# A perceiver's next latents: reads of their PSUM banks moved within VectorE's step, two operations moved to GpSimd, and six banks for the context's products

## The chip, the cores and the metric

The kernel runs on one core of a Trainium2 chip. The metric is the device time of one execution in microseconds (us). Five engines take part, each with its own queue of instructions that it works off in order: TensorE (PE, products, with its weight loads PEld), VectorE (DVE), ScalarE (ACT), GpSimd (POOL) and SyncE (SP, which here only issues transfers). They meet at semaphores: an instruction that has to wait holds up everything behind it in its own queue.

## The reference

Two layers of cross attention and feed forward. The change lies in the second layer's attention, a perceiver: eight batches, 512 latents each (the rows of x after layer 0), 16 heads of 64, a context of 77 rows per batch.

```python
xn = layernorm(x, ln_x_g, ln_x_b)             # context, 8 x 77 rows
ln = layernorm(latents, ln_l_g, ln_l_b)       # 8 x 512 rows of 512
q = ln @ Wq
kv = concatenate((xn, ln), axis=1) @ Wkv      # k, v of context and latents
sim = einsum('bhid,bhjd->bhij', q * scale, k) # masked on the context
out = einsum('bhij,bhjd->bhid', softmax(sim), v)
```

The latents are x plus the output of the feed forward of layer 0, `x2 = x + alpha @ vo + bo`, normalised twice in one go (the layernorm before the attention and the attention's own).

## The kernel before

The kernel is a row of stages; a stage ends before the next begins. Two of them matter.

**The latents stage** (`build_latents`, tiles named `la_`) normalises and transposes the context, computes K and V of the context for all batches, and makes the latents of batch 0 alone (`FIRST = 1`). Every product is made of three passes (high x high, high x low, low x high; lines 119 to 121), since each operand is kept as a high part and a low part: ScalarE copies the result from its PSUM bank rounded ("hi"), and VectorE subtracts that from the bank ("lo"), after which the bank is free. The loop runs over eight pairs of heads: two K products (24 passes of 308 columns), one or two V halves (12 passes of 512 columns), and after the first pair the sixteen transposes of batch 0's latents. `place` (L1381) says which of eight banks a product takes; `claim` makes TensorE wait for the bank's last reader. `Vst` holds one block of V's rows until it has been stored.

**The perceiver stage** (`build_perceiver`, tiles `pa_`) runs 512 steps: 8 batches x 16 heads x 4 tiles of 128 latents; four steps are a head. A step's chain is: scores on TensorE (L1946, L1948, into one of two S buffers), their minimum on VectorE (`least`, L2218), the exponential on ScalarE (L2085), the reciprocal of the sum on VectorE (L2214), and the probabilities scaled on GpSimd (L1875). A head's probabilities are transposed in the next head's steps (T0 to T4, L1959), split into PTh (ScalarE) and PTl (VectorE, L2135), and weigh V (L1975, L1976). Every engine's list is written out step by step, and the order of the code within a step is the order on the engine. Q, K and V of later heads are computed between the steps. Three banks W serve Q, K, V and all transposes: `claim` (L1889 on) takes the bank that was released longest ago and waits for VectorE's mark "read" of its last user.

Beside that the latents of the next batch are made tile by tile, 28 tiles in all. A tile begins every 12 steps, so at an even head (steps 0 and 24 of a batch) or at an odd one (12 and 36). With n0 the step at which it begins: TensorE computes x2 at the end of step n0 (`residual`, L1984); VectorE adds it to x and measures at n0 + 1 (L2185, L2187, L2191); GpSimd makes the inverse root at n0 + 2 (L1881, L1883); VectorE normalises at n0 + 3 (L2196); TensorE transposes at the end of n0 + 4 (L1992); VectorE scales and shifts the result at n0 + 5 (L2202, four pieces); ScalarE rounds it at n0 + 6 (L2118); VectorE makes the low part at n0 + 7 (L2208); ScalarE's queue stores both. In VectorE's step this work stood last:

```python
for late, work in ((-1, ones), (1, add_and_measure), (3, normalised), (5, scaled), (7, latent_low)):
    if tile_at(n, late) is not None:
        work(tile_at(n, late))
```

Of the kernel before, what the change touches and what calls it, by code (L numbers as in the profile page):

```python
# [16 lines left out]
ALU = mybir.AluOpType  # L17
# [1310 lines left out]
def build_latents(nc, orders, a, x1_s, alphaT_s, vo_s, x2_s, z_s, Kc_s, Vc_s, Wkv, ahead):  # L1328
# [15 lines left out]
    with ExitStack() as ctx:  # L1344
# [12 lines left out]
        z_hi, z_lo = two("z_hi", [P, C, T], F32R), two("z_lo", [P, C, T], F32R)  # L1357
# [4 lines left out]
        Vst = sb("V", [P, PAIRS * 2, 2 * HD], F32R)  # L1362
# [7 lines left out]
        K_out, V_out = [sem(f"K_out{m}") for m in range(2)], sem("V_out")  # L1370
# [4 lines left out]
        for n in ("x", "l"):  # L1375
# [5 lines left out]
        place = {"x2": lambda b, t: t, "zT": lambda b, c: 3 + (b * C + c) % 3, "cT": lambda c: 3 + c % 3,  # L1381
                 "cT last": lambda: 4, "K": lambda q, h: 6 + h, "V": lambda k, h: 6 + h}
# [10 lines left out]
        def v_parts(k, h):  # L1393
            r = rows_of(k)
            src = bank_of["V", k, h][0:r, :].rearrange("p (h r d) -> p h r d", r=2, d=HD)
            to = Vst[0:r, h * VH:(h + 1) * VH, :].rearrange("p (h r) (x d) -> p h (r x) d", r=2, d=HD)
            return src, to[:, :, 0:4:3, :], to[:, :, 1:3, :]
# [3 lines left out]
        @block.sync  # L1401
        def _(sp):
            def load_small(b):
                m = b % 2
                sp.dma_start(aT[m][0:NS, :], alphaT_s[b]).then_inc(aT_in[m], 16)
                sp.dma_start(vo[m][0:NS, :], vo_s[b]).then_inc(vo_in[m], 16)

            def keys_out(q):
                for z in range(2):
                    sp.wait_ge(*(act_s, dve_s)[z].after(("hi", "free")[z], "K", q, 1))  # L1410
                    sp.dma_start(Kc_s[z][q], f32(Kst[z][q % 2][:, :])).then_inc(K_out[q % 2], 16)

            def values_out(k):
                sp.wait_ge(*dve_s.after("free", "V", k, 1))
                sp.dma_start(Vc_s[k * P:k * P + rows_of(k), :], f32(Vst[0:rows_of(k), :, :]).rearrange("p h d -> p (h d)"))\
                  .then_inc(V_out, 16)

            load_small(0)
            for dst, src in smalls:
                sp.dma_start(dst, src).then_inc(small, 16)  # L1420
            for b in range(FIRST):
                sp.wait_ge(*dve_s.after("free", "x2", b, NT - 1))
                sp.dma_start(x2_s[b:b + 1].rearrange("b (t p) d -> p (b t) d", p=P), X[b]).then_inc(x2_out[b], 16)
            for b in range(PAIRS):
                keys_out(b)
                for q, h in [i for i in v_of(b) if i[1]]:
                    values_out(q)
            for b in range(FIRST):
                sp.wait_ge(x2_out[b], 16)
            for m in range(2):  # L1430
                sp.wait_ge(K_out[m], 16 * PAIRS)
            sp.wait_ge(V_out, 16 * KT)
# [81 lines left out]
        def _(act):  # L1514
# [30 lines left out]
            for b in range(PAIRS):  # L1545
# [6 lines left out]
                for k, h in v_of(b):  # L1552
                    act.wait_ge(*pe_s.after("V", k, h))
                    if k:
                        act.wait_ge(V_out, 16 * k)
                    src, hi, _ = v_parts(k, h)
                    act.activation(hi, src, ACT.Copy).then_inc(*act_s.mark("hi", "V", k, h))
# [80 lines left out]
def build_perceiver(nc, orders, a, x1_s, alphaT_s, vo_s, x2_s, z_s, Kc_s, Vc_s, o_s, xs_s, mask_s, Wq, Wkv, Wout_s):  # L1638
# [26 lines left out]
    with ExitStack() as ctx:  # L1665
# [188 lines left out]
        def _(pool):  # L1854
# [16 lines left out]
            for n in range(STEPS):  # L1871
# [7 lines left out]
                if i is not None:  # L1879
# [3 lines left out]
                    pool.tensor_tensor(lrstd, lve, minus_half, ALU.pow).then_inc(*pool_s.mark("x2 rstd", i))  # L1883
            low_part(PAIRS - 1)

        @block.tensor
        def _(pe):
# [99 lines left out]
            def latent(i):  # L1987
                u = ("zT", i)
                claim(u)
                pe.wait_ge(*dve_s.after("xn", i))  # L1990
# [37 lines left out]
        def _(act):  # L2028
# [52 lines left out]
            for n in range(1 - LEAD, STEPS + 2 * NT + 1):  # L2081
# [42 lines left out]
                if i is not None:  # L2124
                    act.wait_ge(*dve_s.after("z lo", i))
                    latent_out(1, i)
# [6 lines left out]
        def _(dve):  # L2133
# [49 lines left out]
            def add_and_measure(i):  # L2183
                dve.wait_ge(*pe_s.after("x2", i))
                dve.tensor_tensor(lx[:, :], bank_of["x2", i][:, :], lx[:, :], ALU.add).then_inc(*dve_s.mark("read", "x2", i))  # L2185
                dve.wait_ge(*dve_s.after("read", "x2", i))
                dve.bn_stats(lstats, lx[:, :]).then_inc(*dve_s.mark("x2 stats", i))  # L2187
                dve.wait_ge(*dve_s.after("x2 stats", i))
                if i:
                    dve.wait_ge(*pool_s.after("x2 ve", i - 1))  # L2190
                dve.bn_aggr(lmv, lstats).then_inc(*dve_s.mark("x2 var", i))  # L2191

            def normalised(i):
                dve.wait_ge(*pool_s.after("x2 rstd", i))
                dve.wait_ge(*dve_s.after("x2 var", i))
                dve.tensor_scalar(ln[:, :], lx[:, :], lmv[:, 0:1], lrstd, ALU.subtract, ALU.mult).then_inc(*dve_s.mark("xn", i))  # L2196
# [8 lines left out]

            def latent_low(i):
                dve.wait_ge(*act_s.after("z hi", i))
                dve.tensor_tensor(ln[:, :], ln[:, :], lx[:, :], ALU.subtract).then_inc(*dve_s.mark("z lo", i))  # L2208

            for n in range(1 - LEAD, STEPS + 2 * NT + 2):  # L2210
# [21 lines left out]
                for late, work in ((-1, ones), (1, add_and_measure), (3, normalised), (5, scaled), (7, latent_low)):  # L2232
                    if tile_at(n, late) is not None:
                        work(tile_at(n, late))
# [779 lines left out]
```

## Time and profile before

| | us |
|---|---|
| median of three runs | 2962.92 (2962.76 to 2970.97) |
| the profiled execution | 2963.73 |
| its span | 2961.9 |

| engine | busy us | share of the span |
|---|---|---|
| PE | 2640.8 | 89% |
| PEld | 2175.1 | 73% |
| DVE | 2063.4 | 70% |
| POOL | 1528.8 | 52% |
| ACT | 1500.4 | 51% |

The table of busy times is an average over all stages. The latents stage lies between about 827 and 930 us of the span, the perceiver between about 932 and 2525 us. A row of the timeline gives the start, the duration, the engine, the line, the operation, the names written and read, and, where the engine stood idle before it, for how long and what ended that. Rows of TensorE overlap, because a product's row runs to the modelled end of its last column, and the next begins before.

### The profile page before, as it was taken

Reading aid. Unit: us, or ns where it says so; the run is one execution under the profiler, and the core shown is the slowest. Engines: PE = TensorE matmul, PEld = TensorE weight load, DVE = VectorE, ACT = ScalarE, POOL = GpSimd, SP = SyncE. Lnnn points to the kernel's source line nnn. Section 1 sums busy time; section 2 is a strip of 40 time slices with the busy share of each in tenths; the row PEclk is TensorE's granted clock in tenths of the full one; section 3 lists DMA queues with packets and bytes.
Section 4 is the critical chain, followed back from the end, with each engine's and each line's share of the span. In section 5 each row is a group of like instructions: output and inputs, shape, how many; then the busy total and the mean of one; then the engine's idle time right before and its main releaser. Section 6 shows DMA issues by size and latency. Waiting matters only on the chain. (4 is left out here: it accounts for less than half of the span.)

```text
span 2961.9 us, 41403 instructions
## 1 busy us (share of the span) xinstructions
PE 2640.8 (89%) x14566; PEld 2175.1 (73%) x14566; DVE 2063.4 (70%) x4153; ACT 1500.4 (51%) x2869; POOL 1528.8 (52%) x1184
## 2 busy tenths in 40 slices
PE   6699999986766999999999999999999997799698
PEld 5577777763445888888888888888888886677476
DVE  4577777733532777877878778778787776577656
ACT  2233334331221667666676666766766776111175
POOL 2365444410000666666666666666666665465555
PEclk9899999998888999999999999999999999899899
DMA  5212212224333334343444343434444323567475
GB/s 185 55 53 56 56 55 68 58 64 139 134 121 129 99 99 125 103 119 98 106 119 106 96 125 104 120 98 106 120 106 101 106 54 123 203 239 271 159 275 189
DMA packets 242675, 351.18 MB, mean 119 GB/s; under 512 B 77760, under 2 KB 114755, under 8 KB 236569
## 3 DMA queue, kind: packets, MB, share of 16 engines
q1 hardware_dynamic: 184979, 268.37, 31.2%
q0 software_dynamic: 11680, 45.02, 4.2%
q10 hardware_dynamic: 45810, 35.14, 3.8%
q8 instruction: 117, 1.92, 0.3%
q14 instruction: 89, 0.73, 0.1%
HBM read 172.47 MB, written 156.64 MB: 111 GB/s over the span
## 5 line engine op out<-in xcount | busy, mean ns | idle before, releaser
L1875 POOL TENSOR_SCALAR pa_Pr<-pa_Pr,pa_rs 128x590 f32<-128x590 f32 x512 | 902.3, 1769 | 571.4 <-DVE pa_rs L2214 571.3
L2218 DVE TENSOR_REDUCE pa_least<-pa_S 128x1 f32<-128x590 f32 x512 | 389.5, 761 | 180.2 <-PE pa_S L1948 176.9
L2085 ACT ACTIVATE pa_Pr<-pa_S,pa_least 128x590 f32<-128x590 f32 x512 | 385.3, 752 | 183.8 <-DVE pa_least L2218 163.1
L2135 DVE TENSOR_TENSOR pa_PTl<-pa_W,pa_PTh 128x512 fp32r<-128x512 f32 (+1 forms) x640 | 421.2, 683 | 18.0 <-ACT pa_PTh L2030 14.2
L2030 ACT ACTIVATE pa_PTh<-pa_W 128x512 fp32r<-128x512 f32 (+1 forms) x640 | 368.3, 595 | 88.3 <-PE pa_W L1959 78.5
L1959 PE MATMUL pa_W<-pa_ident,pa_Pr 128*128 128x128 f32 (+1 forms) x2560 | 370.5, 275 | 9.8 <-DVE pa_PTl L2135 8.1
L1959 PEld LDWEIGHTS pa_W<-pa_ident,pa_Pr 128*128 128x128 f32 (+1 forms) x2560 | 303.0, 142 | 39.9 <-DVE pa_PTl L2135 11.0
L1975 PE MATMUL pa_O<-pa_PTh,pa_V 128*128 128x512 f32 (+1 forms) x640 | 290.2, 453 | 23.7 <-DVE pa_PTl L2135 19.6
L1946 PE MATMUL pa_S<-pa_U,pa_Qh 128*128 128x296 f32 (+1 forms) x1024 | 242.3, 318 | 18.2 <-ACT pa_Pr L2085 14.5
L1976 PE MATMUL pa_O<-pa_PTl,pa_V 128*128 128x512 f32 (+1 forms) x640 | 253.3, 396 | 0.0
L1946 PEld LDWEIGHTS pa_S<-pa_U,pa_Qh 128*128 128x128 f32 x1024 | 181.7, 189 | 68.0 <-ACT pa_Pr L2085 26.0
L1948 PE MATMUL pa_S<-pa_Um,pa_Ql 128*128 128x296 f32 (+1 forms) x1024 | 223.6, 300 | 0.0
L514 POOL TENSOR_TENSOR l_E<-l_E,l_rs 128x1232 f32<-128x1232 f32 x32 | 81.1, 2533 | 202.8 <-DVE l_rs L916 202.8
L1948 PEld LDWEIGHTS pa_S<-pa_Um,pa_Ql 128*128 128x128 f32 x1024 | 167.0, 190 | 0.0
L1975 PEld LDWEIGHTS pa_O<-pa_PTh,pa_V 128*128 128x128 f32 (+1 forms) x640 | 121.0, 189 | 56.0 <-DVE pa_PTl L2135 40.6
L119 PE MATMUL pa_W<-Wkv_hi,pa_z_hi 128*128 128x256 f32 x512 | 147.2, 288 | 12.2 <-DVE pa_xn_next L2202 12.2
L121 PE MATMUL pa_W<-Wkv_hi,pa_z_lo 128*128 128x256 f32 x512 | 143.7, 281 | 0.0
L120 PE MATMUL pa_W<-Wkv_lo,pa_z_hi 128*128 128x256 f32 x512 | 143.6, 281 | 0.0
L119 PE MATMUL pa_W<-pa_z_hi,Wq_hi 128*128 128x512 f32 x256 | 108.1, 422 | 29.8 <-DMA pa_z_lo<-z_s 16.0
L2668 ACT ACTIVATE ex_xT_hi<-ex_bank 128x512 fp32r<-128x512 f32 x92 | 53.4, 599 | 145.1 <-PE ex_bank L2564 138.7
L1976 PEld LDWEIGHTS pa_O<-pa_PTl,pa_V 128*128 128x128 f32 (+1 forms) x640 | 122.6, 192 | 4.4
L2214 DVE RECIPROCAL pa_rs<-pa_rs 128x1 f32<-128x1 f32 x512 | 80.9, 158 | 64.5 <-ACT pa_Pr L2085 61.9
(516 smaller groups left out, 6568.0 us busy)
## 6 DMA issues: line engine op xcount, KB each, us to landing
xs_s<-pa_Ql SPq DMA_DIRECT2D x57, 576.0 KB
pa_Um<-pa_U SPq DMA_DIRECT2D x128, 147.5 KB
pa_Qh<-pa_Qh SPq DMA_DIRECT2D x128, 128.0 KB
o_s<-pa_O_hi SPq DMA_DIRECT2D x64, 256.0 KB, 2.3
o_s<-pa_O_sum SPq DMA_DIRECT2D x64, 256.0 KB, 3.0
Wkv_hi<-o_s SPq DMA_DIRECT2D x8, 2048.0 KB, 11.4
Wkv_lo<-o_s SPq DMA_DIRECT2D x8, 2048.0 KB, 17.1
l_xa<-x SPq DMA_DIRECT2D x8, 1024.0 KB, 6.4
```

The costliest lines, as they stand in the source:

```text
L119: pe.matmul(out, a[0], b[0], start=first, stop=False)
L121: return pe.matmul(out, a[1], b[0], start=False, stop=last)
L1875: pool.tensor_scalar(p, p, rs[:, g % 2, t:t + 1], None, ALU.mult).then_inc(*pool_s.mark("probs", n))
L1946: pe.matmul(out[:, a0:a1], qh, U[p % 2][x][:, a0:a1], start=True, stop=False)
L1948: m = pe.matmul(out[:, a0:a1], ql, Um[p % 2][x][:, a0:a1], start=False, stop=True)
L1959: m = pe.transpose(bank_of[u][0:KEYS[c], t * P:(t + 1) * P], Pr[g % 2][:, t, c * P:c * P + KEYS[c]], ident[:, :])
L1975: pe.matmul(Oc[:, :], v, PTh[0:n, r, :], start=(c == 0), stop=False)
L1976: pe.matmul(Oc[:, :], v, PTl[0:n, r, :], start=False, stop=(c == NC - 1)).then_inc(*pe_s.mark("PV", g, c))
L2030: act.activation(out, src, ACT.Copy, scale=scale).then_inc(*act_s.mark("hi", *name))
L2085: act.activation(Pr[g % 2][:, t, :], scored[n % 2], ACT.Exp, scale=-1.0, bias=least[:, g % 2, t:t + 1], accum_out=rs[:, g % 2, t:t + 1]).t ...
L2135: dve.tensor_tensor(out, src, f32(hi_ap), ALU.subtract).then_inc(*dve_s.mark(*name))
L2218: dve.tensor_reduce(least[:, g % 2, t:t + 1], scored[n % 2], AX, ALU.min).then_inc(*dve_s.mark("least", n))
```

## The change

In the latents stage K goes to banks 6 and 7 or 2 and 3 by turns, V to banks 4 and 5, the transposed latents to banks 0 and 1; V's rows get two buffers in turn, and the high and low parts of z one each instead of two.

In the perceiver, VectorE's `add_and_measure` is cut in two: `add` (which reads the x2 bank) and `scaled` (which reads the bank of the transposed tile) now come directly behind `least`; `measure` stays where it was. The normalisation moves from VectorE at n0 + 3 to GpSimd at n0 + 2, behind the inverse root, and the low part from VectorE to GpSimd, both at n0 + 7. TensorE, ScalarE and VectorE wait for GpSimd's marks in the places where they waited for VectorE's.

```diff
-        z_hi, z_lo = two("z_hi", [P, C, T], F32R), two("z_lo", [P, C, T], F32R)
+        z_hi, z_lo = ([sb(n, [P, C, T], F32R)] for n in ("z_hi", "z_lo"))
-        Vst = sb("V", [P, PAIRS * 2, 2 * HD], F32R)
+        Vst = two("V", [P, PAIRS * 2, 2 * HD], F32R)
...
-        place = {"x2": lambda b, t: t, "zT": lambda b, c: 3 + (b * C + c) % 3, "cT": lambda c: 3 + c % 3,
-                 "cT last": lambda: 4, "K": lambda q, h: 6 + h, "V": lambda k, h: 6 + h}
+        place = {"x2": lambda b, t: t, "zT": lambda b, c: c % 2, "cT": lambda c: 3 + c % 3,
+                 "cT last": lambda: 4, "K": lambda q, h: (6, 2)[q % 2] + h, "V": lambda k, h: 4 + h}
...
-                    if k:
-                        act.wait_ge(V_out, 16 * k)
+                    if k >= 2:
+                        act.wait_ge(V_out[k % 2], 16 * (k // 2))
...
                     pool.tensor_tensor(lrstd, lve, minus_half, ALU.pow).then_inc(*pool_s.mark("x2 rstd", i))
+                    pool.wait_ge(*pool_s.after("x2 rstd", i))
+                    pool.tensor_scalar(ln[:, :], lx[:, :], lmv[:, 0:1], lrstd, ALU.subtract, ALU.mult).then_inc(*pool_s.mark("xn", i))
+                i = tile_at(n, 7)
+                if i is not None:
+                    pool.wait_ge(*act_s.after("z hi", i))
+                    pool.tensor_tensor(ln[:, :], ln[:, :], lx[:, :], ALU.subtract).then_inc(*pool_s.mark("z lo", i))
...
-                pe.wait_ge(*dve_s.after("xn", i))
+                pe.wait_ge(*pool_s.after("xn", i))
...
-                    act.wait_ge(*dve_s.after("z lo", i))
+                    act.wait_ge(*pool_s.after("z lo", i))
...
-                    dve.wait_ge(*pool_s.after("x2 ve", i - 1))
+                    dve.wait_ge(*pool_s.after("xn", i - 1))
...
                     dve.tensor_reduce(least[:, g % 2, t:t + 1], scored[n % 2], AX, ALU.min).then_inc(*dve_s.mark("least", n))
+                if tile_at(n, 1) is not None:
+                    add(tile_at(n, 1))
+                if tile_at(n, 5) is not None:
+                    scaled(tile_at(n, 5))
                 for u in evacuated(n - 2):
                     read(u)
...
-                for late, work in ((-1, ones), (1, add_and_measure), (3, normalised), (5, scaled), (7, latent_low)):
-                    if tile_at(n, late) is not None:
-                        work(tile_at(n, late))
+                if tile_at(n, -1) is not None:
+                    ones(tile_at(n, -1))
+                if tile_at(n, 1) is not None:
+                    measure(tile_at(n, 1))
```

The orders below give a line, the operation, the names with their buffer numbers (W0 to W2 are the three banks), and what each waits for. First VectorE in the perceiver around the x2 of an even tile, before: pa_V0 is V's low part, pa_O_sum the head's output, pa_x_next the sum.

```order
L2218 TENSOR_REDUCE pa_least<-pa_S1 128x1 [waits pa_products]
L2135 TENSOR_TENSOR pa_V0<-pa_W1,pa_V0 128x4x128 [waits pa_act]
L2167 TENSOR_TENSOR pa_O_sum<-pa_O,pa_O_sum 64x512 [waits pa_act]
L2185 TENSOR_TENSOR pa_x_next<-pa_W2,pa_x_next 128x512 [waits pa_products]
L2187 BN_STATS pa_norm<-pa_x_next 128x6 [waits pa_dve]
L2191 BN_AGGR pa_norm<-pa_norm 128x2 [waits pa_pool,pa_dve]
```

The same place after.

```order
L2218 TENSOR_REDUCE pa_least<-pa_S1 128x1 [waits pa_products]
L2192 TENSOR_TENSOR pa_x_next<-pa_W2,pa_x_next 128x512 [waits pa_products]
L2142 TENSOR_TENSOR pa_V0<-pa_W1,pa_V0 128x4x128 [waits pa_act]
L2174 TENSOR_TENSOR pa_O_sum<-pa_O,pa_O_sum 64x512 [waits pa_act]
L2196 BN_STATS pa_norm<-pa_x_next 128x6 [waits pa_dve]
L2200 BN_AGGR pa_norm<-pa_norm 128x2 [waits pa_pool,pa_dve]
```

The addition moved ahead of V's low part and the output. TensorE there, after (before it reads the same but for the line numbers): x2 into W2, the scores of the step after, T0 into W0 and T1 into W1, then the query into W2.

```order
L1991 MATMUL pa_W2<-pa_vo,pa_xn_next 128x512 [waits pa_vo_in,pa_dve,pa_x_in]
L1953 MATMUL pa_S0<-pa_U00,pa_Qh00 128x296 [waits pa_act]
L1966 MATMUL pa_W0<-pa_ident,pa_Pr1 128x128 [waits pa_dve,pa_pool]
L1966 MATMUL pa_W1<-pa_ident,pa_Pr1 128x128 [waits pa_dve]
L119 MATMUL pa_W2<-pa_z_hi,Wq_hi 128x512 [waits pa_dve]
```

Nothing moved on TensorE; T1 takes W1, the bank that V's low part reads. On an odd tile that bank is K's. VectorE four steps later, around the scaling of the even tile's transpose (pa_xn_next, from W1; pa_U10 and pa_U11 are K's low parts, from W0), before:

```order
L2218 TENSOR_REDUCE pa_least<-pa_S1 128x1 [waits pa_products]
L2135 TENSOR_TENSOR pa_U10<-pa_W0,pa_U10 64x512 [waits pa_act]
L2135 TENSOR_TENSOR pa_U11<-pa_W0,pa_U11 64x512 [waits pa_act]
L2167 TENSOR_TENSOR pa_O_sum<-pa_O,pa_O_sum 64x512 [waits pa_act]
L2202 TENSOR_SCALAR pa_xn_next<-pa_W1,pa_norm 128x128 [waits pa_products,pa_norm_in]
L2202 TENSOR_SCALAR pa_xn_next<-pa_W1,pa_norm 128x128 x3
```

And after:

```order
L2218 TENSOR_REDUCE pa_least<-pa_S1 128x1 [waits pa_products]
L2206 TENSOR_SCALAR pa_xn_next<-pa_W1,pa_norm 128x128 [waits pa_products,pa_norm_in]
L2206 TENSOR_SCALAR pa_xn_next<-pa_W1,pa_norm 128x128 x3
L2142 TENSOR_TENSOR pa_U10<-pa_W0,pa_U10 64x512 [waits pa_act]
L2142 TENSOR_TENSOR pa_U11<-pa_W0,pa_U11 64x512 [waits pa_act]
L2174 TENSOR_TENSOR pa_O_sum<-pa_O,pa_O_sum 64x512 [waits pa_act]
```

The scaling moved ahead of K's low parts and the output. TensorE's T0 there takes W2 and T1 takes W0, the bank of K; the V product behind them takes W1.

## Rows read from the trace of the kernel before

**Rows 1.** Waits, perceiver, 960 to 2500 us: total us, times, longest us.
```profile
PE pa_W L119 <- DVE pa_xn_next L2202: 26.0, 28, 1.0
...
DVE pa_xn_next L2196 <- POOL pa_norm L1883: 22.1, 14, 1.6
```

**Rows 2.** Timeline, latents stage: VectorE, TensorE, ScalarE.
```profile
849.86 1.92 DVE L1605 TENSOR_SCALAR la_xn<-WihT,la_mv,la_rstd 128x512 f32<-128x512 f32 x4 [1.42 <-POOL la_rstd L1449]
...
852.22 0.79 PE L119 MATMUL la_bank<-Wkv_hi,la_zc_hi 128*128 128x512 f32 x1 [6.52 <-DVE la_K_lo L1621]
...
858.26 2.78 ACT L1533 ACTIVATE la_z_lo<-la_bank,la_lb,la_lg 128x512 f32<-128x512 f32 x4
...
867.84 0.30 PE L119 MATMUL la_bank<-la_zc_hi,Wkv_hi 128*128 128x308 f32 x1
...
871.23 0.39 PE L119 MATMUL la_bank<-Wkv_hi,la_zc_hi 128*128 128x512 f32 x1
...
875.90 0.41 PE L119 MATMUL la_bank<-la_zc_hi,Wkv_hi 128*128 128x308 f32 x1 [1.70 <-DVE la_V L1626]
...
924.65 0.60 ACT L1557 ACTIVATE la_V<-la_bank 104x512 fp32r<-104x512 f32 x1 [2.16 <-PE la_bank L121]
```

**Rows 3.** Windows, latents stage: busy us of each engine, granted clock, DMA share, GB/s.
```profile
852.00:857.50 5.50, 5.28 (x12) 4.03 (x13) 0.55 (x2) 0.00 (x0) 0.00 (x0) 0.50 0.15 57
```

**Rows 4.** Timeline, an even tile (batch 2, step 24 on): TensorE and VectorE.
```profile
1421.87 1.03 PE L1984 MATMUL pa_W<-pa_vo,pa_xn_next 65*128 65x512 f32 x2
...
1423.28 1.04 PE L1959 MATMUL pa_W<-pa_ident,pa_Pr 128*128 128x128 f32 x8
...
1435.42 0.60 PE L1992 MATMUL pa_W<-pa_ident,pa_xn_next 128*128 128x128 f32 x4
...
1436.41 1.19 PE L1959 MATMUL pa_W<-pa_ident,pa_Pr 128*128 128x128 f32 x8
...
1439.07 0.39 PE L119 MATMUL pa_W<-Wkv_hi,pa_z_hi 128*128 128x256 f32 x1 [0.92 <-DVE pa_xn_next L2202]
...
1421.83 0.68 DVE L2135 TENSOR_TENSOR pa_V<-pa_W,pa_V 128x512 fp32r<-128x512 f32 x1
...
1423.31 0.67 DVE L2185 TENSOR_TENSOR pa_x_next<-pa_W,pa_x_next 128x512 f32<-128x512 f32 x1
...
1435.48 1.41 DVE L2135 TENSOR_TENSOR pa_U<-pa_W,pa_U 64x512 fp32r<-64x512 f32 x2
...
1437.65 1.37 DVE L2202 TENSOR_SCALAR pa_xn_next<-pa_W,pa_norm 128x128 f32<-128x128 f32 x4
```

**Rows 5.** Timeline, an odd tile (batch 2, step 12 on): TensorE, VectorE, GpSimd.
```profile
1385.16 1.02 PE L1984 MATMUL pa_W<-pa_vo,pa_xn_next 65*128 65x512 f32 x2
...
1386.58 1.03 PE L1959 MATMUL pa_W<-pa_ident,pa_Pr 128*128 128x128 f32 x8
...
1390.40 0.66 PE L1959 MATMUL pa_W<-pa_ident,pa_Pr 128*128 128x128 f32 x4 [0.58 <-DVE pa_PTl L2135]
...
1396.83 0.50 PE L1975 MATMUL pa_O<-pa_PTh,pa_V 77*128 77x512 f32 x1 [0.53 <-DVE pa_PTl L2135]
...
1400.44 0.51 PE L119 MATMUL pa_W<-pa_z_hi,Wq_hi 128*128 128x512 f32 x1 [1.02 <-DVE pa_xn_next L2202]
...
1385.23 1.41 DVE L2135 TENSOR_TENSOR pa_U<-pa_W,pa_U 64x512 fp32r<-64x512 f32 x2
...
1394.90 0.55 DVE L2196 TENSOR_SCALAR pa_xn_next<-pa_x_next,pa_norm 128x512 f32<-128x512 f32 x1 [1.56 <-POOL pa_norm L1883]
...
1389.17 1.77 POOL L1875 TENSOR_SCALAR pa_Pr<-pa_Pr,pa_rs 128x590 f32<-128x590 f32 x1 [4.29 <-DVE pa_rs L2214]
...
1394.29 0.57 POOL L1883 TENSOR_TENSOR pa_norm<-pa_norm 128x1 f32<-128x1 f32 x1
```

**Rows 6.** Groups by line and shape, GpSimd: count, busy us, mean ns, idle before.
```profile
L1869 POOL TENSOR_TENSOR pa_O_sum<-pa_O_sum,pa_O_hi 128x512 f32<-128x512 f32 x64 | 82.2, 1284 | 10.7 <-ACT pa_O_hi L2103 10.6
...
L485 POOL TENSOR_SCALAR l_xa<-l_xa,l_mv,l_rstd 128x512 f32<-128x512 f32 x32 | 66.6, 2096 | 0.9
```

More of the change, by code:

```diff
@@ L1369, in build_latents @@
         x2_out, z_out = [sem(f"x2_out{r}") for r in range(RING)], [sem(f"z_out{m}") for m in range(2)]
-        K_out, V_out = [sem(f"K_out{m}") for m in range(2)], sem("V_out")
+        K_out, V_out = [sem(f"K_out{m}") for m in range(2)], [sem(f"V_out{m}") for m in range(2)]
         pe_s, act_s, dve_s, pool_s = (Marks(sem(n), orders) for n in ("products", "act", "dve", "rstd"))
@@ L1395, in v_parts @@
             src = bank_of["V", k, h][0:r, :].rearrange("p (h r d) -> p h r d", r=2, d=HD)
-            to = Vst[0:r, h * VH:(h + 1) * VH, :].rearrange("p (h r) (x d) -> p h (r x) d", r=2, d=HD)
+            to = Vst[k % 2][0:r, h * VH:(h + 1) * VH, :].rearrange("p (h r) (x d) -> p h (r x) d", r=2, d=HD)
             return src, to[:, :, 0:4:3, :], to[:, :, 1:3, :]
@@ L1414, in values_out @@
                 sp.wait_ge(*dve_s.after("free", "V", k, 1))
-                sp.dma_start(Vc_s[k * P:k * P + rows_of(k), :], f32(Vst[0:rows_of(k), :, :]).rearrange("p h d -> p (h d)"))\
-                  .then_inc(V_out, 16)
+                sp.dma_start(Vc_s[k * P:k * P + rows_of(k), :], f32(Vst[k % 2][0:rows_of(k), :, :]).rearrange("p h d -> p (h d)"))\
+                  .then_inc(V_out[k % 2], 16)
             load_small(0)
@@ L1431, in _ @@
                 sp.wait_ge(K_out[m], 16 * PAIRS)
-            sp.wait_ge(V_out, 16 * KT)
+            for m in range(2):
+                sp.wait_ge(V_out[m], 16 * len(range(m, KT, 2)))
         @block.gpsimd
@@ L2181, in ones, with add, measure @@
                 dve.memset(alphas[NS:NS + 1, :], 1.0).then_inc(*dve_s.mark("ones", i))
-            def add_and_measure(i):
+            def add(i):
                 dve.wait_ge(*pe_s.after("x2", i))
                 dve.tensor_tensor(lx[:, :], bank_of["x2", i][:, :], lx[:, :], ALU.add).then_inc(*dve_s.mark("read", "x2", i))
+            def measure(i):
                 dve.wait_ge(*dve_s.after("read", "x2", i))
@@ L2189, in add_and_measure @@
                 if i:
-                    dve.wait_ge(*pool_s.after("x2 ve", i - 1))
+                    dve.wait_ge(*pool_s.after("xn", i - 1))
                 dve.bn_aggr(lmv, lstats).then_inc(*dve_s.mark("x2 var", i))
[L2193 to L2196, printed above, removed]
             def scaled(i):
@@ L2204, in scaled @@
                 m.then_inc(*dve_s.mark("read", "zT", i))
-            def latent_low(i):
-                dve.wait_ge(*act_s.after("z hi", i))
-                dve.tensor_tensor(ln[:, :], ln[:, :], lx[:, :], ALU.subtract).then_inc(*dve_s.mark("z lo", i))
             for n in range(1 - LEAD, STEPS + 2 * NT + 2):
```

## The prediction

> **What bounds the kernel now.** I read the waits first, then the timeline of single steps, engine by engine. The change touches two stages: the latents (about 827 to 930 us of the span) and the perceiver (about 932 to 2525 us). TensorE is the busy engine of both, so only what makes TensorE wait, or takes a wait from it, is counted.
>
> In the perceiver TensorE's longest named wait on the latents is for VectorE's scaling of the transposed tile: 26.0 us over 28 tiles [rows 1]. The reader should see in [rows 4, 5] how it arises: VectorE is late with its reads, TensorE needs the same bank for the next product, and stands still 0.92 us (even tiles) or 1.02 us (odd tiles). "Even" is a tile that starts at an even head, "odd" one at an odd head; there are 14 of each. Odd tiles also wait 0.58 and 0.53 us for a low part of the probabilities (L2135), since VectorE works on the tile, or waits for GpSimd, first: 22.1 us in 14 waits [rows 1, 5].
>
> In the latents stage all K and V products share banks 6 and 7. The first V product waits 6.52 us for K's low part, which VectorE does only after measuring and normalising the latents (L1605 ends at 849.86 + 1.92 = 851.78) [rows 2], and after that wait the clock stands at 0.50, the 1.2 GHz level, for 5.5 us [rows 3].
>
> **Latents stage, part by part.** K takes 871.23 - 867.84 = 3.39 us, a V half 875.90 - 1.70 - 871.23 = 2.97 us with its drain, 2.8 without [rows 2]. In the new order V's first half has bank 4, free since the context's transposes. It starts at 852.22 - 6.52 = 845.70 and ends at 848.5. The sixteen transposes of the latents still need L1605, so TensorE waits until 851.8: part of the old stall stays. Their evacuation takes 2.78 us on ScalarE [rows 2] and now goes through two banks, so the next K starts at 854.3 to 855.2. Behind it stand seven K pairs and nine V halves, 7 x 3.39 + 9 x 2.85 = 49.4 us, with no bank in the way: each bank's last reader is more than one product back. The stores are no new bound, since with the second V buffer a store has until the next half but one to land. The stage's last V is ready at 903.7 to 904.6 instead of 924.65 [rows 2]: 20 to 21 us less. If the clock again falls to 0.50 for 5.5 us, because of the 3.3 us pause that stays, half of that, 2.7 us, is lost. I take **-19**, with ends -16 and -21.5. The single buffer for z costs nothing, as only batch 0 is computed here, and the stage's tail is unchanged.
>
> **Perceiver, even tile.** The order on VectorE is what matters: `add` and `scaled` now stand directly behind `least`, ahead of the low part of V or K, and they wait there for products that TensorE issues at the very end of the step before. The bank of that V or K is claimed by the second group of transposes (T1) of the next step, as the bank numbers of the order show.
> - x2: the product ends at 1421.87 + 1.03 = 1422.90. Before, VectorE used this time for V's low part (1421.83). Now it waits, then adds (0.67) and does V's low part (0.68): 1424.25. T1, the second four of eight transposes begun at 1423.28, stood at about 1423.7. **+0.55** [rows 4].
> - Scaling: the transposed tile is ready at 1435.42 + 0.60 = 1436.02; scaling takes 1.37, K's two low parts 1.41: 1438.80. T1 stood at 1436.41 + 0.53 = 1436.94, so it comes 1.9 later. The V product was ready to start at 1439.07 - 0.92 = 1438.15, 1.2 behind T1; now it starts at 1438.85 + 1.2 = 1440.05 instead of 1439.07. The wait of 0.92 is gone, and the longer one ahead of it leaves **+0.95** [rows 4]. Together 1.5, ends 1.2 and 1.7, as the ends of TensorE's rows are good to a few tenths.
>
> **Perceiver, odd tile.** x2 ends at 1385.16 + 1.02 = 1386.18; add and K's low parts, 0.67 + 1.41, end at 1388.26, while T1 stood at 1387.1: 1.2 later. VectorE's whole chain begins at 1386.18 instead of 1385.23, so the transposes at 1390.40 come 0.95 later; their old wait of 0.58 soaks up only the difference [rows 5]. Taking the normalisation (0.55, and 1.56 of waiting for GpSimd) from VectorE removes the wait of 0.53 at 1396.83: the sum is +0.4 [rows 5].
>
> Then GpSimd. Its chain from 1389.17 to the inverse root's end at 1394.86 moves by 0.95 to 1395.81. The normalisation is not in this stage's trace on GpSimd, but the first layer runs the same form there (128x512, subtract and multiply by columns) at 2.10 us [rows 6]. It ends at 1397.9. Behind it waits the last probabilities of the head: 1.77 more [rows 5], 1399.7. TensorE's next transposes stood at 1400.44 - 1.02 - 1.04 = 1398.38 and need them, so the query could start at 1400.75. Behind the tile's own transposes (1397.9 + 0.60), scaling (1.37) and V's low part (0.68) it starts at 1400.55 + 0.5 = 1401.05 against 1400.44. **+0.65**, ends +0.2 and +1.2 [rows 4, 5].
>
> The GpSimd price is the place where a page speaks differently. The Trainium skill, GPSIMD Engine Reference, section 4.1 (Engine selection), calls VectorE the engine for elementwise work, GpSimd about twice as slow with two inputs and roughly at line rate with one. The trace agrees on two inputs (1.28 against 0.68 us) and not on one: 2.10 against VectorE's 0.55 us. By the page's one-input rate the odd tile would cost 0.2 instead of 0.65.
>
> The low part on GpSimd (1.28 us, as L1869 [rows 6]) comes one step ahead of a new wait on ScalarE. Queued behind that wait is the exponential of the step after next, and for it wait VectorE's reciprocal and GpSimd's probabilities. From VectorE's reciprocal on GpSimd needs 1.77 + 1.28 = 3.05 us, and ScalarE arrives after about as long, one step of its own work. I put it at nothing, since what is late by some tenths there is read by TensorE more than a step later; without that cover 0.4 us on each even tile, an estimate from these rows, would be 6 us. Taking the low part from VectorE gives nothing either: no wait of TensorE follows it.
>
> **Sum.** 14 x (0.55 + 0.95 + 0.65) = +30 us in the perceiver, ends 14 x 1.4 = +20 and 14 x 2.9 = +41. With -19 this is +11, ends -2 and +25. The profiled execution took 2963.7 us, so 2974.8; the median of the runs lies 0.8 below it: **2974**.
>
> **Rivals.**
> - *The change does what it says* (faster). The bank waits go and none takes their place: 26.0 + 14 x (0.58 + 0.53) = 41.5 us less [rows 1, 5], and 19: 2902. For it: these are the waits named longest. Against: T1's bank is read behind `add` and `scaled`. It decides if VectorE finds the products done when it arrives. 0.07.
> - *The two parts cancel* (no change). The ends of TensorE's rows are modelled; if x2 and the transposed tile are ready 0.3 us sooner, three of the four new waits shrink by that, and if GpSimd normalises in 0.55 us instead of 2.10, the odd tile costs 0.2. Then the perceiver loses 14 x (0.25 + 0.65 + 0.2) = 15 us to 24 us, and the total is -4 to +5: 2959 to 2968. The page's one-input rate above would put it there. Against: 2.10 is a measured row of the same form. 0.26.
> - *GpSimd becomes the bound* (slower still). If the normalisation also holds back the last probabilities of even heads, or lengthens beside VectorE, the even tile loses another 1.3 us: +18, 2992. It decides where probabilities end after the next head's first transposes. Against: even tiles have no low part of the output (1.28 us) in that place. 0.12.
> - *The forecast*, 2966 to 2985: 0.55.
>
> A difference under 0.3% (9 us) can't be told from none here. Above 2972 lie the last rival and most of the forecast's case: slower 0.64. Same 0.25, faster 0.11. Range: 2957 to 2991.
>
> **What would show it.** In the new profile, TensorE's wait for the scaling (L119 behind it) should be nearly gone, and waits of the transposes (L1959's successor) for VectorE's low parts of V and K should appear: 0.5 to 0.6 and 1.9 us on even tiles, 1.2 us on odd ones. VectorE should show waits for the x2 product and the latent transposes, about 1 and 0.6 us. GpSimd's normalisation should take 2.1 us, and the odd heads' transposes should wait for its probabilities. The latents stage should end near 905 instead of 925, with a pause before the sixteen transposes. The forecast is wrong if T1 does not wait, if the latents stage gains under 15 us, or if GpSimd's work shows as a wait on even tiles.

## The result and the profile after

The changed kernel takes **2996.14 us** (median of 4 runs, 2987.32 to 2999.66), against 2964.52 us for the kernel before on the same chip (4 runs, 2962.76 to 2970.97): a ratio of 1.0098, interval 1.0071 to 1.0125. It is slower, as forecast, but by 32 us instead of 11, and it lies above the range. The profiled execution of the changed kernel is the fastest of its runs, 2987.32 us with a span of 2985.5 us: 23.6 us above the profiled execution of before. The slower runs of the changed kernel have a lower mean granted clock, 0.950 at 2999.66 us against 0.954 in the profiled one.

I read the waits first, as before. TensorE's own in the perceiver, 960 to 2480 us, in the changed kernel (us in total, times, longest):

```profile
PE pa_W L1966 <- DVE pa_U L2142: 43.5, 27, 2.3
PE pa_W L1966 <- DVE pa_V L2142: 11.2, 27, 0.4
PE pa_W L1966 <- DVE pa_PTl L2142: 7.1, 14, 0.5
PE pa_W L1966 <- POOL pa_Pr L1876: 7.0, 14, 0.5
PE pa_O L1982 <- DVE pa_PTl L2142: 6.9, 7, 1.0
PE pa_W L1999 <- POOL pa_xn_next L1886: 4.1, 14, 0.3
PE pa_W L1991 <- DMA pa_vo<-vo_s: 2.4, 4, 1.1
PE pa_W L1991 <- issue: 1.8, 2, 1.7
```

The wait of the products (L119) for the scaling, 26.0 us in [rows 1], is gone. In its place the transposes of the probabilities (L1966, L1959 before) wait for the low parts of K (pa_U) and V (pa_V) that now stand behind the addition and the scaling: 54.7 us. All named waits of TensorE in this stretch sum to 84.0 us; the same view of the kernel before sums to 54.3 us. The difference is 29.7 us. This window leaves out the first even tile of the changed kernel, whose perceiver begins 19.3 us earlier in the span; from the perceiver's first exponential (L2085, L2092 after) to its last, the named waits sum to 104.4 instead of 72.4 us: **32.0 us** more, where the forecast had +30. But the perceiver became longer by more. From its first exponential to its last it takes 1602.3 us instead of 1556.3: **+46 us**.

The even tile, at the place of [rows 4], in the changed kernel's timeline (start, us, engine, line, operation, tiles, and the idle time before it with what ended it). First TensorE, then VectorE:

```profile
1416.12 1.02 PE L1991 MATMUL pa_W<-pa_vo,pa_xn_next 65*128 65x512 f32 x2
...
1418.53 0.66 PE L1966 MATMUL pa_W<-pa_ident,pa_Pr 128*128 128x128 f32 x4 [0.40 <-DVE pa_V L2142]
...
1430.30 0.60 PE L1999 MATMUL pa_W<-pa_ident,pa_xn_next 128*128 128x128 f32 x4
...
1431.29 0.60 PE L1966 MATMUL pa_W<-pa_ident,pa_Pr 128*128 128x128 f32 x4
1433.88 0.74 PE L1966 MATMUL pa_W<-pa_ident,pa_Pr 128*128 128x128 f32 x4 [1.98 <-DVE pa_U L2142]
1434.29 0.81 PE L1953 MATMUL pa_S<-pa_U,pa_Qh 128*128 128x296 f32 x2
...
1435.40 0.41 PE L119 MATMUL pa_W<-Wkv_hi,pa_z_hi 128*128 128x256 f32 x1
...
1417.18 0.69 DVE L2192 TENSOR_TENSOR pa_x_next<-pa_W,pa_x_next 128x512 f32<-128x512 f32 x1 [1.01 <-PE pa_W L1991]
1417.79 0.68 DVE L2142 TENSOR_TENSOR pa_V<-pa_W,pa_V 128x512 fp32r<-128x512 f32 x1
...
1431.02 1.37 DVE L2206 TENSOR_SCALAR pa_xn_next<-pa_W,pa_norm 128x128 f32<-128x128 f32 x4 [0.68 <-PE pa_W L1999]
1432.41 1.41 DVE L2142 TENSOR_TENSOR pa_U<-pa_W,pa_U 64x512 fp32r<-64x512 f32 x2
```

VectorE waits 1.01 us for the x2 product and 0.68 us for the transposed latents. In that time it could have read V or K, whose banks the second four transposes need: these come 0.40 and 1.98 us late. What the forecast did not have is in the next two rows of TensorE. Behind the 1.98 us pause two score products take 0.81 us, and the V product's parts (L119) 0.41 us instead of the 0.28 us that the same form takes at 1382.81 us. The granted clock, in windows of the same place (us; busy us and count of PE, PEld, DVE, ACT, POOL; granted clock; DMA share; GB/s):

```profile
1434.00:1434.30 0.30, 0.30 (x5) 0.30 (x5) 0.30 (x1) 0.00 (x0) 0.00 (x0) 1.00 0.00 0
1434.30:1437.70 3.40, 3.40 (x18) 3.40 (x16) 3.12 (x7) 1.85 (x4) 2.86 (x2) 0.50 0.00 0
```

For 3.4 us the clock stands at 0.50, the 1.2 GHz level. This happens behind 8 of the 14 pauses of the even tiles in this execution (1.98 us each, but for one of 2.33 and the first of 1.28 us), and nowhere in the perceiver of before between 963.5 and 2489 us. The four steps of a head with such a fall take 15.4 us from exponential to exponential, without it 13.85 us: 1.55 us each, **12.4 us** in all. With the 32.0 us of waits that is 44.4 of the 46 us; the other 1.6 us are not assigned.

The perceiver of before has one such fall too, just behind its first exponentials, after a wait of 3.23 us for the weights of x2 (pa_vo). Its longest wait from there to 2489 us is 1.21 us, for the same weights, with no fall behind it. The two waits, and the window behind the first:

```profile
959.15 1.10 PE L1984 MATMUL pa_W<-pa_vo,pa_xn_next 65*128 65x512 f32 x2 [3.23 <-DMA pa_vo<-vo_s]
...
1739.48 1.10 PE L1984 MATMUL pa_W<-pa_vo,pa_xn_next 65*128 65x512 f32 x2 [1.21 <-DMA pa_vo<-vo_s]
```

```profile
960.20:963.50 3.30, 3.30 (x11) 2.79 (x10) 2.28 (x5) 0.83 (x2) 1.43 (x1) 0.50 0.00 0
```

An odd tile, at the place of [rows 5], TensorE and GpSimd:

```profile
1381.76 0.66 PE L1966 MATMUL pa_W<-pa_ident,pa_Pr 128*128 128x128 f32 x4 [1.25 <-DVE pa_U L2142]
1384.88 0.66 PE L1966 MATMUL pa_W<-pa_ident,pa_Pr 128*128 128x128 f32 x4 [0.50 <-DVE pa_PTl L2142]
1391.54 0.63 PE L1999 MATMUL pa_W<-pa_ident,pa_xn_next 128*128 128x128 f32 x4 [0.28 <-POOL pa_xn_next L1886]
1393.22 0.66 PE L1966 MATMUL pa_W<-pa_ident,pa_Pr 128*128 128x128 f32 x4 [0.49 <-POOL pa_Pr L1876]
1394.30 0.66 PE L1966 MATMUL pa_W<-pa_ident,pa_Pr 128*128 128x128 f32 x4 [0.43 <-DVE pa_V L2142]
...
1389.31 2.08 POOL L1886 TENSOR_SCALAR pa_xn_next<-pa_x_next,pa_norm 128x512 f32<-128x512 f32 x1
1391.38 5.39 POOL L1876 TENSOR_SCALAR pa_Pr<-pa_Pr,pa_rs 128x590 f32<-128x590 f32 x3
```

Five waits, 2.95 us, stand where three, 0.58 + 0.53 + 1.02 = 2.13 us, stood before [rows 5].

The latents stage, TensorE, ScalarE and VectorE, at the place of [rows 2]:

```profile
848.33 0.39 PE L119 MATMUL la_bank<-Wkv_hi,la_zc_hi 128*128 128x512 f32 x1
...
853.33 4.44 PE L1468 MATMUL la_bank<-la_ident,la_xn 128*128 128x128 f32 x16 [2.03 <-DVE la_xn L1606]
...
906.77 0.60 ACT L1558 ACTIVATE la_V<-la_bank 104x512 fp32r<-104x512 f32 x1 [2.16 <-PE la_bank L121]
...
852.64 1.92 DVE L1606 TENSOR_SCALAR la_xn<-WihT,la_mv,la_rstd 128x512 f32<-128x512 f32 x4 [1.42 <-POOL la_rstd L1450]
```

The first V product starts at once, a pause of 2.03 us stays ahead of the sixteen transposes, and the last V is evacuated at 906.77 instead of 924.65 us. The stage began 2.7 us later in this execution (its first product at 835.88 against 833.14 us), so it is 17.9 + 2.7 = 20.6 us shorter. Part of that is a pause that the forecast did not name, though its sum of products leaves it out: before, TensorE waited 3.89 us for V's low part at 890.36 us, since ScalarE had waited 4.68 us for a store of V, and the clock stood at 0.50 from 888.5 to 895.3 us. After, neither is there.

### The profile page after: what moved, and what is told of

Its sections match the earlier page's. It is cut to its first block and busy times, and to the rows that moved or that the text cites. A ratio compares the mean times of both kernels' runs of the same rounds, so it can differ in the third digit from the quotient of the medians.

```text
span 2985.5 us, 41373 instructions
## 1 busy us (share of the span) xinstructions
PE 2651.8 (89%) x14566; PEld 2183.8 (73%) x14566; DVE 2035.9 (68%) x4097; ACT 1506.5 (50%) x2869; POOL 1623.1 (54%) x1240
## 5 line engine op out<-in xcount | busy, mean ns | idle before, releaser
L1966 PE MATMUL pa_W<-pa_ident,pa_Pr 128*128 128x128 f32 (+1 forms) x2560 | 383.9, 277 | 71.2 <-DVE pa_U L2142 44.8
L2092 ACT ACTIVATE pa_Pr<-pa_S,pa_least 128x590 f32<-128x590 f32 x512 | 385.2, 752 | 117.7 <-DVE pa_least L2218 92.1
L1966 PEld LDWEIGHTS pa_W<-pa_ident,pa_Pr 128*128 128x128 f32 (+1 forms) x2560 | 302.9, 143 | 115.6 <-DVE pa_U L2142 51.4
L119 PE MATMUL pa_W<-Wkv_hi,pa_z_hi 128*128 128x256 f32 x512 | 148.0, 289 | 0.0
L2037 ACT ACTIVATE pa_O_sum<-pa_O 64x512 f32<-64x512 f32 x128 | 75.8, 592 | 94.3 <-PE pa_O L1983 61.3
## 6 DMA issues: line engine op xcount, KB each, us to landing
Wkv_lo<-o_s SPq DMA_DIRECT2D x8, 2048.0 KB, 17.1
```

The lines of the kernel that those rows point to most:

```text
L119: pe.matmul(out, a[0], b[0], start=first, stop=False)
L1966: m = pe.transpose(bank_of[u][0:KEYS[c], t * P:(t + 1) * P], Pr[g % 2][:, t, c * P:c * P + KEYS[c]], ident[:, :])
L2037: act.activation(out, src, ACT.Copy, scale=scale).then_inc(*act_s.mark("hi", *name))
L2092: act.activation(Pr[g % 2][:, t, :], scored[n % 2], ACT.Exp, scale=-1.0, bias=least[:, g % 2, t:t + 1], accum_out=rs[:, g % 2, t:t + 1]).t ...
```

## The experiments

Unless said otherwise an edit is made to the changed kernel. "Perceiver" is the time between its first and last exponential in the profiled execution; "falls" are falls of the granted clock behind one of the fourteen even pauses, or in their place.

| kernel | median us (range, runs) | ratio to before (95%) | perceiver us | falls |
|---|---|---|---|---|
| before | 2964.52 (2962.76 to 2970.97, 4) | | 1556.3 | 0 |
| changed | 2996.14 (2987.32 to 2999.66, 4) | 1.0098 (1.0071 to 1.0125) | 1602.3 | 8 |
| e0, the same again | 2989.45 (2986.28 to 3000.93, 4) | 1.0080 (1.0053 to 1.0107) | 1605.7 | 8 |
| e1, pause filled | 2980.67 (2976.54 to 2983.97, 4) | 1.0045 (1.0029 to 1.0062) | 1589.7 | 0 |
| e8, half filled | 2981.07 (2976.80 to 2984.66, 7) | 1.0029 (1.0016 to 1.0043) | 1595.0 | 0 |
| e2, scaling put back | 2957.50 (2953.26 to 2967.99, 7) | 0.9972 (0.9955 to 0.9989) | 1571.9 | 0 |
| e4, addition put back | 2959.75 (2956.07 to 2964.75, 6) | 0.9965 (0.9953 to 0.9978) | 1571.7 | 2 |
| e5, both put back | 2937.59 (2934.19 to 2940.31, 4) | 0.9893 (0.9875 to 0.9912) | 1549.2 | 0 |
| e6, early but behind the reads | 2938.55 (2935.36 to 2944.05, 4) | 0.9901 (0.9880 to 0.9922) | 1548.1 | 0 |
| e3, latents stage alone | 2944.01 (2942.94 to 2951.92, 4) | 0.9926 (0.9906 to 0.9946) | 1558.4 | 0 |
| e7, e3 and the scaling moved up | 2942.90 (2937.50 to 2946.05, 4) | 0.9905 (0.9885 to 0.9926) | 1554.6 | 0 |
| e9, perceiver alone | 3007.10 (3004.55 to 3014.10, 4) | 1.0122 (1.0101 to 1.0142) | 1600.5 | 6 |
| e10, e5 and the scaling moved up | 2939.77 (2934.87 to 2942.94, 4) | 0.9885 (0.9868 to 0.9901) | 1549.1 | 0 |

Three groups of kernels ran on three chips, each beside runs of the kernel before: 2966.84 us for e0 to e3, 2968.34 us for e4 to e7, 2971.61 us for e8 to e10. The first two rows were measured together, apart from these. Between groups the ratios are the fairer comparison.

**e0, the changed kernel once more.**

> The changed kernel once more, to see how its time spreads. Theory A (the clock): TensorE's pauses of 1.98 us at the even tiles (T1 waiting for K's low parts behind the scaling) let the granted clock fall to 0.50 for 3.4 us in some of the 14 tiles, and each fall costs about 1.5 us; the profiled execution had 8 such falls at 2987.3 us, so executions near 2997 should have about 14, and one with none would take 2975. Theory B (something else varies, a transfer or another stage): the number of falls in the perceiver does not go with the time.

The falls come back: 8 again, though only in part behind the same tiles, and a ninth elsewhere (1747.4 us, behind a wait of 1.23 us for the weights of x2). The loss is smaller, 24 us by the ratio instead of 29, and the two intervals overlap. Since only one execution of each kernel has a trace, it is not shown that the number of falls follows the time from run to run.

**e1, the pause filled with products.**

```
-                    transposed(g - 1, 0)
+                    transposed(g - 1, 0, tile_at(n, 5) is not None and n % LEAD == 5)
...
+                if c == 0 and fill:
+                    for _ in range(FILL):      # FILL = 15
+                        pe.matmul(bank_of[u][:, 0:256], z[0][:, 0, 0:P], Wkv[0][:, 0, 0:256], start=True, stop=True)
```

> At the 14 even tiles TensorE does 15 extra products of 256 columns (their result is overwritten) into the bank of T0 ahead of T0, so it works through most of the pause of 1.98 us in front of T1; all waits and all order on the other engines stay. Theory A (the clock falls because TensorE pauses): no fall to 0.50 inside the perceiver, the wait in front of T1 about 0.2 to 0.4 us, time 2973 to 2978 us and a narrow spread. Theory B (the clock is not what makes the runs slower than 2975): 2987 to 2997 as before. If the extra products are simply more work: 14 x 1.8 = 25 us on top, 3010 to 3020.

TensorE around the same even tile in this kernel:

```profile
1418.09 0.66 PE L1969 MATMUL pa_W<-pa_ident,pa_Pr 128*128 128x128 f32 x4 [0.40 <-DVE pa_V L2145]
1433.41 0.66 PE L1969 MATMUL pa_W<-pa_ident,pa_Pr 128*128 128x128 f32 x4 [0.20 <-DVE pa_U L2145]
```

The extra products take the time in which TensorE stood still, so the transposes come no sooner; only the clock no longer falls. The perceiver is 12.6 us shorter than in the changed kernel and 33.4 us longer than before. So this one kernel separates the two terms: about 33 us are the waits, which the forecast put at 30, and about 12 us the clock, which it did not have. The median is 2.7 us above the expected 2973 to 2978; the mechanism holds in the profiled executions. The medians say it less sharply: e1 is 8.8 us faster than e0 on the same chip, and their intervals overlap. By the ratios of e1 and e8 against those of the changed kernel and e0 the clock is worth 1.0080 to 1.0098 less 1.0029 to 1.0045, some 10 to 20 us.

**e2, the scaling back behind the output; the addition stays early.**

```
                 if tile_at(n, 1) is not None:
                     add(tile_at(n, 1))
-                if tile_at(n, 5) is not None:
-                    scaled(tile_at(n, 5))
...
                     measure(tile_at(n, 1))
+                if tile_at(n, 5) is not None:
+                    scaled(tile_at(n, 5))
```

> Only the scaling goes back to its old place on VectorE, behind K's or V's low part and the output. Theory A: the wait of 1.98 us in front of T1 goes, the old 0.92 us in front of V comes back, which is 0.95 us less for each even tile and some 0.3 us less for each odd one, and no clock falls: 2975 - 13 - 4 = 2958 (2952 to 2964). Rival (GpSimd's share is what costs, not VectorE's order): the falls and most of the loss stay, above 2978.

The perceiver is 30.4 us shorter than in the changed kernel, the 1.98 us pauses are gone, and so are the falls. The median, 2957.50 us, is what theory A gave.

**e3, the latents stage alone.** The kernel before with the change's banks, V buffers and single z buffers of that stage.

> Only the six banks of the context's products and V's second buffer; the perceiver as before. By the two traces the stage's products end 20.7 us sooner after its start: 2964.5 - 21 = 2943 us (2941 to 2947). Rival (what the stage gains is given back at the perceiver's start, by stores that come in a shorter time): 2950 to 2960.

Some 22 us faster than before, by the interval 16 to 28. The stage is worth what its own term said.

**e4, the addition back behind the output; the scaling stays early.** The edit is that of e2 with `add(tile_at(n, 1))`.

> Only the addition of x2 goes back to its old place behind V's or K's low part and the output; the scaling stays early. If the waits in front of T1 come from VectorE waiting for the x2 product: 0.4 us on even tiles and about 0.95 on odd ones go, 14 x 1.35 = 19 us, while the wait of 1.98 us behind the early scaling and the clock's falls stay: 2990 - 19 = 2971 us (2964 to 2980), with some falls to 0.50 in the perceiver. Rival (the early addition costs little, the loss is GpSimd's): above 2982.

2959.75 us is 11 us under the expectation and below its range. From the first exponential to the last the named waits sum to 83.8 us, 20.6 less than in the changed kernel, where 19 was expected. The rest is the clock. All the long pauses are still there, but the clock falls behind 2 of the 14 (958.1 and 1354.1 us; the expectation of e8 below counts from the second tile on, and so one) instead of 8; six falls fewer are 9.3 us. Two of these pauses in this kernel, and the windows behind them:

```profile
1353.60 0.71 PE L1966 MATMUL pa_W<-pa_ident,pa_Pr 128*128 128x128 f32 x4 [1.98 <-DVE pa_U L2142]
...
1430.94 0.66 PE L1966 MATMUL pa_W<-pa_ident,pa_Pr 128*128 128x128 f32 x4 [1.98 <-DVE pa_U L2142]
```

```profile
1354.10:1357.50 3.40, 3.40 (x18) 3.40 (x17) 3.04 (x7) 1.85 (x4) 2.94 (x2) 0.50 0.00 0
1433.00:1436.40 3.40, 3.40 (x26) 3.17 (x26) 2.93 (x6) 2.55 (x6) 3.40 (x3) 1.00 0.20 73
```

Two pauses of 1.98 us, equal in the trace, one with the clock at 0.50 behind it and one at 1.00 (and at 1.00 from the pause's end to that window too). So the pause alone does not decide.

**e5, both back behind the output.** What is left in the perceiver is the normalisation and the low part on GpSimd.

> Addition and scaling both back in their old places; what is left of the change in the perceiver is the normalisation and the low part on GpSimd. It prices GpSimd's part alone, beside the kernel with the latents stage alone (2944 us). By the rows: the wait of 0.53 us on odd tiles goes, and GpSimd's longer chain (2.1 us more ahead of the last probabilities) gives back about as much: 2944, from 2938 to 2952. Rival (GpSimd's two operations are a loss of their own, by its port or its lateness): above 2955.

TensorE's waits in the perceiver, 960 to 2480 us, in this kernel:

```profile
...
PE pa_W L119 <- DVE pa_xn_next L2206: 12.0, 13, 0.9
PE pa_W L1966 <- DVE pa_PTl L2142: 8.1, 14, 0.6
PE pa_O L1982 <- DVE pa_PTl L2142: 7.8, 8, 1.0
PE pa_W L1966 <- POOL pa_Pr L1876: 7.1, 14, 0.5
PE pa_W L1999 <- POOL pa_xn_next L1886: 6.1, 14, 0.4
...
```

The transposes' waits for K and V are gone altogether: the early place of the addition and the scaling is what made them. The loss divides as follows. With neither early the perceiver takes 1549.2 us, with the addition alone 1571.9, with the scaling alone 1571.7 (two falls, 3 us of it), with both and no falls 1589.7: 23, 20 and 40 us. And what stays, GpSimd's work, looks like a small gain and not the break-even that was expected: 9.2 us in the perceiver against e3, 6.4 us in the medians (the two intervals just overlap). The wait of an odd tile's product for the scaling (1.02 us) and the low part's wait of 0.53 us are gone, 14 of each; GpSimd's own two waits, 13.2 us together, take back part of it.

**e6, both early, but behind the reads of K and V.** The order on VectorE is then the smallest score, the reads, the addition, the scaling, the output.

```
+                for u in evacuated(n - 2):
+                    read(u)
                 if tile_at(n, 1) is not None:
                     add(tile_at(n, 1))
                 if tile_at(n, 5) is not None:
                     scaled(tile_at(n, 5))
-                for u in evacuated(n - 2):
-                    read(u)
```

> All of the change, but VectorE does the low parts of V or K first, then addition and scaling, then the output: early, yet behind the read that T1 needs. If VectorE waiting in front of that read is the whole loss, no T1 wait is left, the wait of the query on odd tiles shrinks by about 0.6 us and no clock falls: 2931 to 2944 us. Rival (the early place itself is bad, since the output and the minimum come later): 2955 or more.

As expected, no wait of the transposes for K or V is left, no clock falls in the place of the even pauses, and the time is 2938.55 us: by the ratios 58 us under the changed kernel and 53 under e0, with four lines in another order. Of the even tile's old wait for the scaling little is left, but the low part of the probabilities now comes late instead; TensorE's waits of 960 to 2480 us:

```profile
PE pa_W L1966 <- DVE pa_PTl L2142: 21.9, 27, 1.0
...
PE pa_W L119 <- DVE pa_xn_next L2206: 2.5, 13, 0.2
```

Against e5 (8.1 and 12.0 us) one wait is exchanged for the other; the time is the same.

**e7, the latents stage, and the scaling behind the reads but ahead of the output; all the rest as before.**

> A candidate: the latents stage of the change, the perceiver as before (normalisation and low part on VectorE), but the scaling stands behind the low parts of V or K and ahead of the output. By the rows before, VectorE is then never early: the odd tile's query starts 0.7 us sooner, the even tile gains about 0.2, since the transposes behind it wait for VectorE anyway: 2944 - 14 x 0.9 = 2931 us (2928 to 2940). Rival (the gain is eaten by the later output): 2944.

Not to be told from e3; the expected 2931 is missed, and the rival's 2944 stands. The products' waits for the scaling shrink from 25.8 us in e3 to 8.1 us, but the transposes wait 17.1 instead of 8.1 us for the low part of the probabilities: half of the gain is gone at once, and the rest is too small to be measured here.

**e8, seven extra products instead of fifteen.** FILL = 7 in e1.

> The changed kernel with seven extra 256-column products, instead of fifteen, into the bank of the first transposes ahead of them at the fourteen even tiles; the transposes overwrite them, so the output is unchanged. Fifteen took the 1.98 us pause down to 0.2 us, so one takes about 0.12 us and seven leave about 1.1 us, still a pause as long as the 1.25 us ones of the neighbouring steps. Theory (the length of the single pause decides whether the granted clock falls): no trace so far shows a fall at a pause of 1.75 us or less, so there is none here either, and the time is that of the fifteen products, 2977 to 2984 us. Rival (the pauses of the whole neighbourhood decide together, as the one fall among fourteen equal pauses with the addition put back suggests): one to five of the eight falls stay, 2982 to 2989 us.

The even tiles wait 1.17 us, and the clock falls behind none of the 14. But it falls at two other places. One of them, TensorE and the window behind it:

```profile
1360.20 0.66 PE L1969 MATMUL pa_W<-pa_ident,pa_Pr 128*128 128x128 f32 x4 [1.17 <-DVE pa_U L2145]
...
1543.47 1.10 PE L1994 MATMUL pa_W<-pa_vo,pa_xn_next 65*128 65x512 f32 x2 [1.25 <-DMA pa_vo<-vo_s]
```

```profile
1544.50:1547.50 3.00, 3.00 (x15) 2.87 (x14) 2.86 (x7) 0.87 (x2) 0.06 (x1) 0.50 0.00 0
```

A wait of 1.25 us for the weights of x2 at the start of a batch is enough there (the other is at 2148.7 us, behind 1.24 us), while the odd tiles' 1.25 us are not in any of these traces. The time is that of e1, as the theory said, but its reason, the length of the single pause, falls. It had been wrong when it was written: e0's trace already shows the fall behind 1.23 us of the same wait. e9 has one as well, behind 1.42 us.

**e9, the perceiver's part alone.** The latents stage is that of before.

> The kernel before with the change in the perceiver alone; the latents stage is that of before. Theory (the two parts add up): the changed kernel's 2989 to 2996 us and the 21 us that the latents stage gave, 3010 to 3017 us, with the perceiver at 1600 to 1606 us from its first to its last exponential and several falls of the granted clock in it. Rival (part of the loss in the perceiver comes from the latents stage that is ahead of it, for example through the clock): perceiver under 1595 us, total under 3005 us.

The perceiver is as expected (1600.5 us), so its loss does not come from the stage ahead of it. The median is 2.9 us under the expected range. That the two parts add up is not settled by it: in the profiled executions e9 takes 3007.2 us, 19.9 us more than the changed kernel, as the latents stage's own term says, but by the ratios it is 7 us more, or 12 against e0, and these intervals overlap.

**e10, e5 with the scaling behind the reads but ahead of the output.**

> The changed kernel with the addition back in its old place behind the output, and the scaling behind the low parts of V and K but ahead of the output; normalisation, low part and latents stage as changed. Theory (only what TensorE waits for counts): the scaling is done no earlier where K's low parts come first, its wait of 0.92 us shrinks by some 0.1 us only, and the time is that of the kernel with both in their old places, 2935 to 2940 us. Rival (an early scaling is worth something if it does not stand ahead of the reads): 2930 us or less.

The time is as expected and not to be told from e5, but not for the reason given. TensorE's waits, 960 to 2480 us:

```profile
PE pa_W L1966 <- DVE pa_PTl L2142: 16.4, 27, 0.6
...
PE pa_W L119 <- DVE pa_xn_next L2206: 2.7, 14, 0.2
```

The wait for the scaling does not shrink by 0.1 us but nearly goes (12.0 us in e5), and the transposes' wait for the low part of the probabilities doubles (8.1 us in e5): one wait is exchanged for the other, as in e6. That the time came out right is luck.

Of all kernels here e5, e6 and e10 have the lowest medians: 1.0 to 1.15% under before, and about 2% under the changed one. e7 can't be told from them.

## Why the prediction was wrong

**The step that failed** is the sentence that only what makes TensorE wait, or takes a wait from it, is counted. A new wait of TensorE has a second price: the granted clock can be at 0.50 for the 3.4 us that follow. The prediction used this itself in the latents stage, from [rows 3], and did not ask it of the new pauses in the perceiver, though it put one of them at 1.9 us. The trace of before raises the question in the perceiver itself: no fall stands behind its waits of up to 1.21 us, and one of 3.4 us stands behind its wait of 3.23 us. A new pause of 1.9 us lies between the two. Priced at the rate of [rows 3], half of 5.5 us, a fall behind each of fourteen pauses is an end of +38 us; eight falls and 12.4 us came of it. The profiled execution is 12.5 us above the forecast for it (2987.3 against 2974.8), so there the falls are about the whole miss, and the errors of the other terms nearly cancel. The median lies 8.8 us higher still, in runs without a trace; that more falls make this up is not shown. A range that took the end of +38 us in would have held the result.

**Even tile, right.** Forecast +0.55 and +0.95, together 1.5; measured 0.40 and 1.98 - 0.92 = 1.06, together 1.46. T1 was put 0.55 and 1.9 us late and is 0.40 and 1.98.

**Odd tile, right in kind, a little low.** Forecast +0.65, measured 2.95 - 2.13 = +0.82. K's low parts hold T1 up by 1.25 us (put at 1.2), the old 0.58 stays as 0.50, and GpSimd's probabilities come 0.49 us late. What was not put down: V's low part holds up the next four transposes by 0.43 us behind that.

**The sum of the waits**, then, is 14 x (1.46 + 0.82) = 32 us against a forecast of 30. The named waits of the whole perceiver are 32.0 us more, and e1 shows 33 without the falls.

**GpSimd.** The normalisation was put at 2.10 us from a row of another stage with the same form [rows 6]. The groups of the changed kernel by line and shape (count, busy us, mean ns, idle before):

```profile
L1886 POOL TENSOR_SCALAR pa_xn_next<-pa_x_next,pa_norm 128x512 f32<-128x512 f32 x28 | 58.3, 2083 | 3.1
...
L1890 POOL TENSOR_TENSOR pa_xn_next<-pa_xn_next,pa_x_next 128x512 f32<-128x512 f32 x28 | 36.1, 1291 | 0.0
```

2.08 and 1.29 us: the rows of the other stage were the right price. The Trainium skill, GPSIMD Engine Reference, section 4.1 (Engine selection), calls one-input work there roughly line rate; the trace disagrees for this form, 2.08 us against VectorE's 0.55 us [rows 5]. The low part at nothing was right: no wait of TensorE follows it, and e5 against e3 shows the two moves together as a gain in the perceiver (9.2 us in the profiled executions). That gain the prediction had only as a part of its odd tile, not as a term of its own.

**Latents stage, right.** Forecast -19, with 20 to 21 us before the clock's share; measured -20.6, and e3 alone is 22 us faster. The pause that stays is 2.03 us and not 3.3, since the transposes start behind the first of the four normalisations, and the clock falls for 3.4 us and not for 5.5.

**The rivals.** The change did not do what it says (2902): T1's bank is read too late, as the rival's own "against" said. The two parts did not cancel. GpSimd did not become the bound: even tiles behind the first show no wait for it, and without the early addition and scaling its work gains. The result's size came from a case that was not among them.

## What to carry to other kernels

On an engine that works in order, an instruction that is moved up takes its own wait with it: what is behind it must be read too, and if one of these reads frees a PSUM bank that the waited-for engine needs next, the wait comes back to that engine, longer. Put the reads that free banks first, and then the work that waits; here four lines in that order are worth 53 to 58 us. And a new pause of TensorE is to be priced twice, once as time and once with half of what it does in the next few us, wherever it is longer than the pauses behind which the trace shows the clock unchanged. The second price is an end of the range and not a sure term: here equal pauses came with and without a fall.

## What the hardware showed that was not expected

The clock's falls are not a matter of one pause. Each lasts 3.4 us at 0.50 and costs 1.55 us here. They stood behind 8, 8 and 6 of the 14 even tiles' pauses in the changed kernel, in its repetition and in e9, but behind 2 of 14 in e4, where the pauses are as long (1.98 us, one of 2.33), with the addition back in its place and no wait of 0.40 us of the transposes 15 us ahead of the pause. They stood behind four waits of 1.23 to 1.42 us for the weights of x2 (e0, e8 twice, e9), but not behind others as long (1.32 us in e0, 1.42 in e6), and behind none of the 14 waits of 1.25 us in the odd tiles of the changed kernel, e0, e1, e2, e8 and e9. What besides the pause decides was not settled by these runs. e4 against the changed kernel suggests that it lies around the pause, but that rests on one traced execution of each kernel.

How much a kernel's runs differ does not tell whether it has these falls: 12 us in the changed kernel and 15 us in its repetition, 7 and 8 us in e1 and e8, but also 15 us in e2 and in the ten runs of before beside e8, whose traces show none behind the even pauses.
